# Attention on one core: the probabilities divided by their sum on GpSimd before they are transposed, and the values held as stationary operand

## The reference, cut to what matters

```
k_all = jnp.concatenate([kc, k], axis=1)          # 512 cached + 32 own keys
v_all = jnp.concatenate([vc, v], axis=1)
scores = jnp.einsum('bqhd,bkhd->bhqk', q, k_all) * SCALE
scores = jnp.where(valid[:, None, None, :], scores, -1e+30)
probs = jax.nn.softmax(scores, axis=-1)
o = jnp.einsum('bhqk,bkhd->bqhd', probs, v_all)
```

## Time and profile before

| what | us |
|---|---|
| median of three runs | 2720.36 (2719.5 to 2720.91) |
| the profiled execution, its own time | 2722.63 |
| its span, first to last instruction | 2720.6 |
| attention, first to last unit (first DVE split of keys at 952.76, last DVE division at 2208.40) | about 1256 |

### The profile page before, as it was taken

The page is one execution under the profiler, slowest core; times in us unless marked ns, Lnnn a source line. Parts: engine busy times, 40 slices in busy tenths (PEclk is TensorE's granted clock), DMA queues, the critical chain, the costliest instruction groups (busy, mean ns, idle before and its releaser), DMA issues. The chain is left out here.

```text
span 2720.6 us, 53012 instructions
## 1 busy us (share of the span) xinstructions
PE 2540.0 (93%) x15632; PEld 2139.9 (79%) x15632; DVE 1867.8 (69%) x3327; ACT 1282.3 (47%) x3654; POOL 808.8 (30%) x743
## 2 busy tenths in 40 slices
PE   2479899999998899999999999999999979999989
PEld 1453588777776689999999999999999967777733
DVE  5242599999995088888888888888888854444311
ACT  1101355555553256666666666666666641111100
POOL 3070166666663022222222222222222231212000
PEclk9689999999998999999999999999999989999989
DMA  5441133332334478888888888888888844343212
GB/s 193 162 158 62 58 96 109 94 95 93 112 93 138 146 251 272 295 271 290 276 290 273 291 274 292 274 286 279 288 277 286 280 149 124 108 123 108 62 69 79
DMA packets 432385, 508.52 MB, mean 187 GB/s; under 512 B 39860, under 2 KB 352468, under 8 KB 431828
## 3 DMA queue, kind: packets, MB, share of 16 engines
q1 hardware_dynamic: 395476, 373.71, 41.9%
q0 software_dynamic: 36864, 134.23, 15.5%
HBM read 407.07 MB, written 100.75 MB: 187 GB/s over the span
## 5 line engine op out<-in xcount | busy, mean ns | idle before, releaser
L1079 PE MATMUL ps<-at_v_raw,at_pt 128*128 128x128 f32 x4096 | 541.1, 275 | 0.6 <-DMA at_v_raw<-v_cache,at_idx 0.6
L1079 PEld LDWEIGHTS ps<-at_v_raw,at_pt 128*128 128x128 f32 x4096 | 497.7, 192 | 1.0 <-DMA at_v_raw<-v_cache,at_idx 1.0
L1179 ACT ACTIVATE at_pt<-ps 128x512 f32<-128x512 f32 x512 | 305.1, 596 | 339.8 <-PE ps L1063 326.1
L1146 DVE CUSTOM_DVE_ANT_0 at_sm<-ps,at_mask 128x544 f32<-128x544 f32 x512 | 367.9, 719 | 91.3 <-PE ps L1054 45.4
L868 POOL TENSOR_TENSOR pr_m<-pr_qn,tb 128x256 f32<-128x256 f32 x320 | 331.6, 1056 | 311.7 <-DVE pr_qn L837 296.5
L1190 ACT ACTIVATE at_pr<-at_sm,at_nm 128x544 f32<-128x544 f32 x512 | 383.9, 750 | 72.1 <-DVE at_nm L1146 59.5
L1017 POOL DMA_INDIRECT at_v_raw<-v_cache,at_idx x256 | 307.5, 1201 | 113.1 <-issue 62.3
L702 PE MATMUL ps<-pr_hi,xh 128*128 (+1 forms) x768 | 319.8, 416 | 13.1 <-DVE pr_lo L691 8.7
L1139 DVE TENSOR_TENSOR at_k_lo<-shared,at_k_hi 128x1088 fp32r<-128x1088 f32 x256 | 325.5, 1272 | 0.0
L1054 PE MATMUL ps<-at_k_hi,at_q_hi 128*128 128x272 f32 x1024 | 295.9, 370 | 13.5 <-DVE at_k_lo L1139 13.5
L1063 PE MATMUL ps<-constants,at_pr 128*128 128x128 f32 x2048 | 307.9, 273 | 0.0
(11 more groups left out here) (197 smaller groups left out, 4423.1 us busy)
## 6 DMA issues: line engine op xcount, KB each, us to landing
shared<-k_t SPq DMA_DIRECT2D x1024, 128.0 KB, 4.3
qk_t<-pr_stage SPq DMA_DIRECT2D x160, 256.0 KB, 2.3
shared<-qk_t SPq DMA_DIRECT2D x64, 512.0 KB, 7.7
o_t<-at_ot SPq DMA_DIRECT2D x64, 512.0 KB, 5.9
o_raw<-o_t SPq DMA_DIRECT2D x32, 1024.0 KB, 5.9
w_first<-wqkv SPq DMA_DIRECT2D x12, 1024.0 KB, 5.9
s_k_in<-k_cache SPq DMA_DIRECT2D x16, 512.0 KB, 7.2
k_t<-s_k_out SPq DMA_DIRECT2D x16, 512.0 KB, 6.3
```

The lines of the kernel that those rows point to most:

```text
L1079: last = e.matmul(ps[:, 5 + w, k * D:(k + 1) * D], pt[:, r, c * P:(c + 1) * P], v_raw[:, q, c, g * D:(g + 1) * D], start=(k == 0 and c == ...
L1146: e.tensor_tensor_reduce(out=halves(sm[:, r, :]), in0=ps[:, 2 * r:2 * r + 2, 0:W], in1=halves(mask[:, q, :]), scale=-SC, scalar=3e38, op0= ...
L1179: e.activation(pt[:, r, :], ps_w, ACT.Copy).then_inc(s_pt, 1)
```

## The change: what it does

- The reciprocal of the row sum moves from once in four units (128x4, phase 6) to once in each unit (128x1, phase 5, ahead of L1146 of the next unit on DVE, and it waits there for the unit's exponential).
- POOL then multiplies the unit's 128x544 probabilities in place by that reciprocal, with one tensor_scalar whose scalar is a column of 128 values. This is new work; 512 of them.
- The four indirect DMAs of a sequence are no longer issued together: POOL issues one in each of the first four steps of a sequence, behind that step's multiplication. The wait for the buffer becomes a wait for the last cached-value matmul of the sequence two before (s_pv).
- All that follows the exponential moves one step later: transposition of probabilities from phase 6 to 7, cached values from 7 to 8, own values from 8 to 9. The pipeline is 12 steps deep instead of 11.
- The matmuls with values swap operands: the values are stationary, the transposed probabilities move. The output comes out as [head width, query]. The own-value matmul, one of 512 columns before, becomes four of 128 columns, one for each unit.
- DVE's multiplication of the output (L1125), the four output transpositions on PE (L1093) and the tile o_n go. ACT copies the output from bank 5 or 6 directly, and the next user of that bank waits for this copy (s_o).

```
@@ gpsimd (once: copy of indices and four gathers per sequence)
-                with e.Fori(0, B // 2 - 1) as i:
-                    for q in range(2):
-                        b = i * 2 + q
-                        wait_apart(e, s_passed[0], (s_nw, (b + 1) * 2))
-                        indices(b + 2, q)
-                        wait_apart(e, s_passed[0], (s_idx, b + 3))
-                        gather_values(q)
+                def step(i, j, u, live):
+                    if live(5):
+                        m, jj = u - 5, j - 5
+                        k, w = jj % QU, (jj // QU) % 2
+                        at = slice(w * QU + k, w * QU + k + 1)
+                        wait_apart(e, s_passed[0], (s_ri, m + 1))
+                        e.tensor_scalar(pr[:, w, k, :], pr[:, w, k, :], ri[:, at], None, ALU.mult).then_inc(s_n, 1)
+                    if live(j % UB) and j % UB < KC:
+                        gather_values(i * 2 + j // UB, (j // UB) % 2, j % UB)
+                steps(e, step)
...
+                def gather_values(b, q, c):
+                    if c == 0:
+                        wait_apart(e, s_passed[0], (s_pv, b - 1))
+                        cols = slice(b * KC, (b + 1) * KC) if isinstance(b, int) else bass.ds(b * KC, KC)
+                        e.tensor_copy(idx[:, q, :], rows[:, cols]).then_inc(s_idx, 1)
+                        wait_apart(e, s_passed[0], (s_idx, b + 1))
+                    e.indirect_dma_start(out=v_raw[:, q, c, :], ...).then_inc(s_vr[q], 16)
@@ tensor
-                        e.wait_ge(s_e, m + 1)
+                        e.wait_ge(s_n, m + 1)
                         for c in range(KC):
                             last = e.transpose(ps_w[:, c * P:(c + 1) * P], pr[:, w, k, c * P:(c + 1) * P], ident)
...
+                        if k == 0:
+                            wait(e, s_o, i * 4 + jj // QU)
                         for c in range(KC):
-                            last = e.matmul(ps[:, 5 + w, k * D:(k + 1) * D], pt[:, r, c * P:(c + 1) * P],
-                                            v_raw[:, q, c, g * D:(g + 1) * D],
+                            last = e.matmul(ps[:, 5 + w, k * P:(k + 1) * P], v_raw[:, q, c, g * D:(g + 1) * D],
+                                            pt[:, r, c * P:(c + 1) * P],
...
-                        e.matmul(ps[:, 5 + w, :], pt_new[:, w, :], v_new[:, q, g // QU, :],
-                                 start=False, stop=True, skip_group_check=True).then_inc(s_nw, 1)
...
-                        e.wait_ge(s_on, i * 4 + jj // QU + 1)
                         for k in range(QU):
-                            last = e.transpose(ps_x[:, k * P:(k + 1) * P], o_n[:, w, k * D:(k + 1) * D], ident)
-                        last.then_inc(s_tr, 1)
+                            last = e.matmul(ps[:, 5 + w, k * P:(k + 1) * P], v_new[:, q, g // QU, k * D:(k + 1) * D],
+                                            pt_new[:, w, :], start=False, stop=(k == QU - 1), skip_group_check=True)
+                        last.then_inc(s_nw, 1)
@@ vector
-                        e.reciprocal(ri[:, mine], su[:, mine]).then_inc(s_ri, 1)
-                    if live(9) and (j - 9) % QU == QU - 1:
...
-                        e.tensor_tensor(o_n[:, w, :].rearrange("p (k d) -> p k d", d=D),
-                                        ps[:, 5 + w, :].rearrange("p (k d) -> p k d", d=D),
-                                        spread(ri[:, w * QU:(w + 1) * QU], 2, D), ALU.mult).then_inc(s_on, 1)
+                    if live(5):
...
+                        e.wait_ge(s_e, m + 1)
+                        e.reciprocal(ri[:, at], su[:, at]).then_inc(s_ri, 1)
@@ scalar
-                        e.wait_ge(s_tr, i * 4 + jj // QU + 1)
-                        e.activation(ot[:, q, t * QU * P:(t + 1) * QU * P], ps_x, ACT.Copy).then_inc(s_o, 1)
+                        e.wait_ge(s_nw, i * 4 + jj // QU + 1)
+                        e.activation(ot[:, q, t * QU * P:(t + 1) * QU * P], ps[:, 5 + t, :], ACT.Copy).then_inc(s_o, 1)
```

More of the change, by code:

```diff
@@ L934, in attention @@
         pt_new = sb("pt_new", [P, 2, P])
-        o_n = sb("o_n", [P, 2, QU * D])
         ot = sb("ot", [P, 2, UB * P])
         s_rows = sem("rows")
-        s_in, s_v, s_one, s_idx, s_mask, s_qhi, s_qlo, s_hi, s_lo, s_s, s_max, s_e, s_ri, s_nc, s_c, s_cn, s_pt, s_wn, s_nw, s_on, s_tr, s_o = (
-            sem(n) for n in ("in", "v", "one", "idx", "mask", "qhi", "qlo", "hi", "lo", "s", "max", "e", "ri", "nc", "c", "cn",
-                             "pt", "wn", "nw", "on", "tr", "o"))
+        s_in, s_v, s_one, s_idx, s_mask, s_qhi, s_qlo, s_hi, s_lo, s_s, s_max, s_e, s_ri, s_n, s_nc, s_c, s_cn, s_pt, s_wn, s_pv, s_nw, s_o = (
+            sem(n) for n in ("in", "v", "one", "idx", "mask", "qhi", "qlo", "hi", "lo", "s", "max", "e", "ri", "n", "nc", "c", "cn",
+                             "pt", "wn", "pv", "nw", "o"))
         s_passed = [sem("passed_pool"), sem("passed_vector")]
@@ L944, in attention @@
         ps_w, ps_x = ps[:, 4, :], ps[:, 7, :]
-        steps = lambda e, step: turns(e, B * UB, PER, 11, step)
+        steps = lambda e, step: turns(e, B * UB, PER, 12, step)
         halves = lambda x: x.rearrange("p (h w) -> p h w", h=2)
@@ L980, in store @@
                 def store(b, q):
-                    e.wait_ge(s_o, (b + 1) * 2)
+                    e.wait_ge(s_o, (b + 1) * 2 + 1)
                     dst = o_t[bass.ds(b, 1), :, :] if not isinstance(b, int) else o_t[b:b + 1, :, :]
@@ L1013, in _ @@
                 e.memset(mask[:, :, :], 0.0).then_inc(s_one, 1)
[L1015 to L1023, removed]
@@ L1025, in _ @@
-                e.wait_ge(s_rows, 1)
-                for q in range(2):
-                    indices(q, q)
-                    e.wait_ge(s_idx, q + 1)
-                    gather_values(q)
-                with e.Fori(0, B // 2 - 1) as i:
-                    for q in range(2):
-                        b = i * 2 + q
-                        wait_apart(e, s_passed[0], (s_nw, (b + 1) * 2))
-                        indices(b + 2, q)
-                        wait_apart(e, s_passed[0], (s_idx, b + 3))
-                        gather_values(q)
+                def gather_values(b, q, c):
[4 more added lines that the diff above has]
+                        wait_apart(e, s_passed[0], (s_idx, b + 1))
+                    e.indirect_dma_start(out=v_raw[:, q, c, :], out_offset=None, in_=dram["v_cache"],
+                                         in_offset=bass.IndirectOffsetOnAxis(ap=idx[:, q, c:c + 1], axis=0)).then_inc(s_vr[q], 16)
@@ L1056, in step @@
                         last.then_inc(s_s, 1)
-                    if live(6):
-                        m, jj = u - 6, j - 6
+                    if live(7):
+                        m, jj = u - 7, j - 7
                         k, w = jj % QU, (jj // QU) % 2
-                        e.wait_ge(s_e, m + 1)
+                        e.wait_ge(s_n, m + 1)
                         wait(e, s_pt, m)
@@ L1064, in step @@
                         last.then_inc(s_c, 1)
-                    if live(7) and (j - 7) % QU == QU - 1:
-                        jj = j - 7
+                    if live(8) and (j - 8) % QU == QU - 1:
+                        jj = j - 8
                         w = (jj // QU) % 2
-                        wait(e, s_o, i * 4 + jj // QU)
+                        wait(e, s_wn, i * 4 + jj // QU)
                         e.wait_ge(s_nc, i * 4 + jj // QU + 1)
                         e.transpose(ps_x[:, 0:P], pr_new[:, w, :], ident).then_inc(s_cn, 1)
-                    if live(7):
-                        m, jj = u - 7, j - 7
+                    if live(8):
+                        m, jj = u - 8, j - 8
                         g, q, r, k, w = jj % UB, (jj // UB) % 2, jj % 2, jj % QU, (jj // QU) % 2
@@ L1076, in step @@
                             e.wait_ge(s_vn[q], (i + jj // PER) * 16 * QU + 16 * QU)
+                        if k == 0:
+                            wait(e, s_o, i * 4 + jj // QU)
                         e.wait_ge(s_pt, m + 1)
                         for c in range(KC):
-                            last = e.matmul(ps[:, 5 + w, k * D:(k + 1) * D], pt[:, r, c * P:(c + 1) * P],
-                                            v_raw[:, q, c, g * D:(g + 1) * D],
+                            last = e.matmul(ps[:, 5 + w, k * P:(k + 1) * P], v_raw[:, q, c, g * D:(g + 1) * D],
+                                            pt[:, r, c * P:(c + 1) * P],
                                             start=(k == 0 and c == 0), stop=False, skip_group_check=True)
-                    if live(8) and (j - 8) % QU == QU - 1:
-                        jj = j - 8
+                        if g == UB - 1:
+                            last.then_inc(s_pv, 1)
+                    if live(9) and (j - 9) % QU == QU - 1:
+                        jj = j - 9
                         g, q, w = jj % UB, (jj // UB) % 2, (jj // QU) % 2
```

(23 more changed lines are left out.)

## The result

The changed kernel takes 2925.4 us (median of four, 2923.8 to 2926.6) against 2720.6 for the kernel before on the same chip: ratio 1.0752, interval 1.0734 to 1.0771. It is 205 us slower. I had forecast 3018 with a range of 2835 to 3140: the direction and the range hold, the size was taken too large by 93 us.

A forecast was written before the change was run, and what follows sets the result against it. PE bound the kernel before, at 19.49 us a sequence; POOL and DVE excluding each other would make it 24.1. Times 64 that is +295 us, plus about 3 for a pipeline step: 3018 us, range 2835 to 3140.

The forecast's parts named there:

- PE's 55 us: Attention, PE: dropping the output transpositions saves 0.43 us in four units, 128 times; counts only if PE stays the bound.
- The multiplication's own price: POOL's new tensor_scalar over 544 elements: 1.58 us each, interpolated from one-operation rows; eight make 12.6 us a sequence.
- ACT and DVE by themselves at nothing: Attention: ACT's same work from other banks costs zero; DVE's sum stays about the same, below PE's.
- exclusive sum: Attention, per sequence: POOL's 12.6 us of multiplications and DVE's 9.0 of all-SBUF instructions cannot overlap, together 21.7 us.
- rival A: Multiplication does not exclude DVE; POOL's queue alone sets the pace, 20.5 us a sequence, about 2788 us; chance 0.10.
- 21.7: Period in us a sequence if POOL and DVE exclude each other and all further lone time is hidden; low bound.
- 24.1: Forecast period in us a sequence, taken a little above the middle of 21.7 and 25.7.
- lonely pieces: Attention: stretches when nobody holds the port, 0.8 us in steps without a gather plus 3.2 with one, a sequence.
- Gathers held by L1139: A POOL gather issued during DVE's L1139 waits for its end: 1.77 us against 0.97 beside nothing.
- Rival B: POOL's multiplication runs at the short price, about 0.6 us; PE stays the bound, 2668 us; chance 0.07.
- C: Rival: PE, idle about a fifth of the time, gets a lower clock; 3160 us and more; chance 0.05.

The follow-up runs named there:

- e1: The changed kernel with POOL's multiplication cut to one column of 544, all waits kept: 2666.5 us, ratio 0.9796 to the kernel before.
- e3: The changed kernel with DVE's two key splits cut in the loop from 1088 elements to 64: 2724.7 us, ratio 1.001 to the kernel before.
- e4: The changed kernel with POOL's multiplication written as two operations, multiply and add 0.0: 2679.7 us, ratio 0.9848 to the kernel before.
- e7: The changed kernel with a sequence's four gathers issued together behind the first step's multiplication: 3051.0 us, ratio 1.1214 to the kernel before.
- e5: The changed kernel with the multiplication moved from POOL to ACT (even units) and DVE (odd units): 2746.8 us, ratio 1.0094 to the kernel before.
- e2: The changed kernel with one gather of four in the loop, the multiplication whole: 2723.2 us, ratio 1.0002 to the kernel before.
- e8: The changed kernel with POOL's multiplication written as multiply, then maximum with 0.0: 3032.1 us, ratio 1.1146 to the kernel before.

## Why the prediction was right, and where it was not

- **PE's 55 us**: right, by e1 (2721.8 - 2666.5).
- **The multiplication's own price**, 1.58 us: right, 1.63 at the shortest. ACT and DVE by themselves at nothing: right, by e1.
- **The term that was mis-sized is the exclusive sum.** "A DVE instruction that takes all its operands from SBUF and a POOL elementwise instruction exclude each other for their whole length" failed: 0.57 us of 1.63 are exclusive. L1127 stayed at 1.29 us where I expected two to three times its length. The sum charged 12.6 us for POOL and 9.0 for DVE; the trace has POOL's whole queue at 18.6 to 19.0, which I gave to rival A at 20.5, then 3.0 of holding and 1.1 of waiting for the reciprocal. That 21.7 lies near the true 22.7 is luck. The 24.1 that I took for the period stands 1.4 above it. It adds 2.4 us of lonely pieces to that sum, and since the sum itself was wrong, the runs don't show what those pieces are worth. The row to see the exclusion in stood ahead of me: L434 ran from 200.50 to 205.87, but L522 behind it was over at 204.29. I read that it was held and did not ask until when.
- **Rival A** was right that POOL's queue sets the pace, and wrong that nothing would be held. With nothing held its queue would have been shorter than the old period, by e3, and not 1.0 us longer.
- **Gathers held by L1139**: right, and by more (mean 1.40 after, 1.20 before). L1140, with its scores in PSUM, was not held (716 ns, 719 before): right. The row that I had for it, L385, did not show it, since it had begun 0.03 us before L136.
- **Rival B** was out for the form in the change and is right in e4: the price is in the form. The estimate of 0.6 us was 0.72.
- **C**: the clock fell only from 1.00 to 0.97 in the attention; with gaps of 3.99 us it was 0.91 (e7).

The Trainium skill (SBUF — State Buffer, section Who interferes with whom) says that whoever comes first has the shared pair for the whole instruction. These rows disagree for POOL's one-input tensor_scalar, which lets DVE go after 0.57 of 1.63 us. For L296 with two inputs they agree: it ends at 41.80, and L141 behind it at 42.21, 0.4 us later. Its rule that one-input elementwise work runs near line rate on GpSimd (GPSIMD Engine Reference, section 4.1 Engine selection) fits e4's 0.72 us and not the 1.63 and 2.09 of the other two forms (DVE's own tensor_scalar over the same 544 columns takes 0.50 us in e5).

## What to carry to other kernels

Before work is given to an idle engine, write that engine's queue for one period with every gap between its instructions, and compare it with the period. Here it came to 18.6 to 19.0 us beside the 18.6 that PE needs. Nothing was lost by that alone, but no slack was left either, so that each piece of holding and waiting, 4.1 us, went straight into the period; in e4, with slack, the same 0.57 us of holding goes with a loss of 13 us in all. Read from a held instruction not only that it was held but at which moment it was let go. And look for the same operation in another form in the trace before pricing it: one more operation in the instruction turned 205 us lost into 42 won.

## What the runs showed that I had not expected

- On POOL a tensor_scalar over 128x544 f32 takes 1.63 us with multiply alone, 0.72 with multiply and add, 2.09 with multiply and maximum.
- It holds DVE for 0.57 to 0.58 us from its start in all three forms, whatever their length.
- Fewer gathers made each multiplication longer (e2, 2.04 us), and with a longer multiplication each gather was shorter (e8, 1.16): what one instruction is held less, others can be held more.
